# Second half of the attention product with V moved ahead of the FFN's value projection

## What is computed

```python
x = layernorm(x + causal_attention(x))          # 16 heads of 16, keys and queries of rank 32
x = layernorm(x + cross_attention(x, ctx))      # 120 context rows, masked after the softmax
x = layernorm(x + ffn(x))                       # r = sigmoid(xr @ W_r.T); k = relu(xk @ W_k.T)**2
                                                # out = r * (k @ W_v.T); xr, xk mix x with the row before
```

## Time and profile before

| | |
|---|---|
| median of 3 runs | 938.26 us (938.09 to 940.07) |
| the profiled execution | 941.16 us, its span from first to last instruction 939.5 us |
| busy share of the span | PE 94%, PEld 77%, DVE 72%, ACT 64%, POOL 47% |
| mean granted TensorE clock | 0.974 |
| chain that ended last | PE 84%, DVE 4%, issue 3%, POOL 2%, DMA 2%, ACT 2% |

### The profile page before, as it was taken

One profiled execution on the slowest core, in us unless ns is written; L12 is line 12 of the kernel. 1 busy time (PEld: TensorE's weight loads), 2 busy tenths in 40 slices (PEclk: granted clock), 3 DMA queues, 4 the chain that ended last, 5 costly groups with the idle time before them and its releaser, 6 DMA issues.

```text
span 939.5 us, 25990 instructions
## 1 busy us (share of the span) xinstructions
PE 883.4 (94%) x9686; PEld 727.9 (77%) x9686; DVE 677.5 (72%) x1565; ACT 598.3 (64%) x1153; POOL 438.7 (47%) x665
## 2 busy tenths in 40 slices
PE   4679899999999999999999999999999999988985
PEld 4557688888888888888888888888888888877765
DVE  2345777778878778777887877877788787776542
ACT  1114467766667667776666766777666676667643
POOL 3001345455455545545545554545545555444553
PEclk8779999999999999999999999999999999999998
DMA  7987667788766667778876667678887676551000
GB/s 210 157 149 137 131 129 138 153 155 155 135 105 134 142 138 141 140 154 156 153 125 111 141 134 143 139 143 154 155 154 109 116 151 137 124 78 29 27 12 23
DMA packets 121880, 120.14 MB, mean 128 GB/s; under 512 B 28249, under 2 KB 105243, under 8 KB 121627
## 3 DMA queue, kind: packets, MB, share of 16 engines
q1 hardware_dynamic: 121755, 118.47, 65.6%
HBM read 75.05 MB, written 42.99 MB: 126 GB/s over the span
## 4 chain that ended last, share of the span: by engine, by line
PE 84%; DVE 4%; issue 3%; SPq 2%; POOL 2%; DMA 2%; ACT 2%; ACTq 0%; POOLq 0%; DVEq 0%
PE ps_m L514 21%; PE ps_m L506 14%; PE ps_s L527 9%; PE ps_o L608 9%; PE ps_t L527 6%; PE ps_s L540 4%; PE ps_m L477 4%; PE ps_m L664 4%; PE ps_m L486 3%; PE ps_m L694 3%; PE ps_m L681 3%; PE ps_m L494 3%; PE ps_t L540 1%; DVE row_max L932 1%; DMA x_in<-in_x_turned 1%
## 5 line engine op out<-in xcount | busy, mean ns | idle before, releaser
L932 DVE TENSOR_REDUCE row_max<-ps_s 128x4 f32<-128x1024 f32 (+1 forms) x192 | 234.8, 1223 | 117.0 <-PE ps_s L540 114.7
L732 ACT ACTIVATE p<-ps_t 128x1024 f32<-128x1024 f32 x192 | 196.3, 1022 | 48.0 <-PE ps_t L540 47.7
L1115 POOL TENSOR_TENSOR xT_lo<-x_in,xT_hi 128x512 fp32r<-128x512 f32 x32 | 42.5, 1329 | 181.6 <-ACT xT_hi L719 181.6
L527 PE MATMUL ps_s<-stack 51*128 51x128 f32 (+1 forms) x1024 | 107.9, 310 | 10.2 <-DVE row_max L932 5.0
L527 PEld LDWEIGHTS ps_s<-stack 51*128 51x128 f32 x1024 | 72.4, 188 | 43.9 <-issue 15.3
L608 PE MATMUL ps_o<-p,v_pad 128*32 128x256 f32 (+1 forms) x2048 | 97.4, 331 | 0.2 <-ACT p L732 0.2
L841 ACT COPY kxT<-ps_m 128x240 f32<-128x240 f32 x32 | 11.5, 358 | 132.8 <-PE ps_m L486 132.8
L527 PE MATMUL ps_t<-stack 53*128 53x128 f32 (+1 forms) x1024 | 91.5, 278 | 2.8 <-DMA stack<-shift_dram 1.4
L608 PEld LDWEIGHTS ps_o<-p,v_pad 128*32 128x32 f32 x2048 | 58.0, 110 | 39.7 <-issue 17.9
L1140 POOL TENSOR_TENSOR var<-mv,eps 128x2 f32<-128x2 f32 x96 | 18.7, 195 | 146.4 <-DVE mv L955 145.7
L527 PEld LDWEIGHTS ps_t<-stack 53*128 53x128 f32 x1024 | 73.9, 189 | 4.8 <-ACT p L732 2.2
(11 more groups left out here) (168 smaller groups left out, 2689.9 us busy)
## 6 DMA issues: line engine op xcount, KB each, us to landing
stack<-parts_dram SPq DMA_DIRECT2D x384, 128.0 KB, 5.7
parts_dram<-parts SPq DMA_DIRECT2D x64, 512.0 KB, 6.0
x_in<-in_x_turned SPq DMA_DIRECT2D x32, 256.0 KB, 8.2
x_res<-in_x SPq DMA_DIRECT2D x32, 256.0 KB, 5.5
out_x<-sum SPq DMA_DIRECT2D x64, 128.0 KB, 6.4
ctxT<-in_ctx_turned SPq DMA_DIRECT2D x32, 120.0 KB, 5.4
shift_dram<-shift_turned SPq DMA_DIRECT2D x64, 16.0 KB
stack<-shift_dram SPq DMA_DIRECT2D x64, 16.0 KB
```

What stands on the lines that cost most here:

```text
L527: nc.tensor.matmul(target[:, at_h:at_h + width], left[b.slot][r0:r0 + rows_n, h // 2, rows_at:rows_at + P], right[b.slot][r0:r0 + rows_n, ...
L732: nc.scalar.activation(p[c][:], ps_t[:], ACT.Exp).then_inc(exp_done[c], 1)
L932: nc.vector.tensor_reduce(row_max[:, :, j0:j0 + nj, tile], ps_s[:].rearrange("p (g j w) -> p g j w", j=nj, g=2), AX_X, ALU.max) \
L1115: g.tensor_tensor(xT[b.slot][1][:], x_in[:], xT[b.slot][0][:].bitcast(F32), ALU.subtract) \
```

## The change

On TensorE `PV(1)` moves from behind z2 to behind g, that is past v3 and z2. On VectorE `attention_out(1)` moves from the end of the step to directly behind `attention_out(0)`, that is past `gated`, `sum2` and the statistics of `sum2`. On ScalarE the rounding `yT_hi` moves from the beginning of the next step to the end of the same step, ahead of the copies of kx and vx. Nothing is added to the work or taken from it.

```diff
                     last.then_inc(filled["f_g"], 1)
                 filler(7, ffn_last)
+                PV(1)
                 if on[FFN]:
                     bank = bank_free(pe, "v3", at)
...
                 filler(16, cross_last)
-                PV(1)
                 if on[PROBS]:
                     bank = bank_free(pe, "kx", at)
...
-                if on[CROSS]:
-                    act.wait_ge(y_turned[0], X.n + 1)
-                    act.wait_ge(y_turned[1], X.n + 1)
-                    wait(act, filled["f_z1"], X.n)
-                    nc.scalar.copy(flat(yT[0]), flat(y32T)).then_inc(a_["yT_hi"], 1)
                 X1, F1 = Batch(at - 1, CROSS), Batch(at - 1, FFN)
                 exp(0)
...
                 x_hi(at + 1)
+                if on[PROBS]:
+                    act.wait_ge(y_turned[0], Pb.n + 1)
+                    act.wait_ge(y_turned[1], Pb.n + 1)
+                    wait(act, filled["f_z1"], Pb.n)
+                    nc.scalar.copy(flat(yT[0]), flat(y32T)).then_inc(a_["yT_hi"], 1)
                 if on[PROBS]:
                     act.wait_ge(filled["f_kx"], Pb.n + 1)
...
                 attention_out(0)
+                attention_out(1)
                 if on[FFN]:
                     dve.wait_ge(filled["f_v3"], F.n + 1)
...
                 if on[CROSS]:
                     stats(1, X, sum2, v_["sum2_done"])
-                attention_out(1)
```

## The result

| | before | after |
|---|---|---|
| median of 17 runs each | 938.81 us (936.80 to 948.12) | 947.66 us (944.81 to 954.28) |
| ratio of the two, 95% interval | | 1.0087 [1.0070, 1.0105] |
| the profiled execution, its span | 941.16, 939.5 us | 948.0, 946.3 us |
| mean granted TensorE clock | 0.974 | 0.978 |
| one step in the steady part, from kx to kx | 26.14 us | 26.42 us |

The change makes the kernel 0.87% slower by the ratio, 8.2 us on 938.8; the two medians are 8.9 us apart. The spans of two single profiles differ by the set-up as well (the first kx starts between 80.5 and 84.1 us, in no relation to the kernel), so lengths are compared from kx to kx: the start of the last kx stands 810.9 us behind that of the first before (83.8 to 894.7) and 820.3 after (81.5 to 901.7).

The account below looks back on a forecast made before the run. The prediction took TensorE's row of products to bound the kernel. Per step, 0.10 us won at v3 less 0.41 us of new wait at kx gave +0.31; 29 x 0.31 = 9.0 on 938.26 made 947.3 us, range 944 to 953.

Parts of the forecast that it names:

- The wait that it named: On TensorE ahead of kx: a new wait for `gated` to read v3's bank, 0.41 us a step.
- The 0.10 us at v3: On TensorE: v3 no longer waits for `r_tanh`, since `PV(1)` covers it, worth -0.10 us a step.
- VectorE's row: On VectorE: `attention_out(1)` starts at 423.84, then `gated` follows at 425.67 and ends at 426.36.
- The term of 0.31 us a step: At kx: 0.10 us won at v3 less 0.41 us of new wait gives +0.31 a step, bounds +0.21 to +0.43.
- What was held to be covered: vx's wait for `sum2` covered by 0.3 us, `offset` by 1.3, `yT_lo` by 1.4; the earlier `yT_hi` costs nothing.
- Step 4: The step without v3: expected within -0.2 to +2 us and taken at nothing.
- The sum: Over steps 5 to 33: 29 x 0.31 = 9.0 us, added to 938.26 to give 947.3 us.
- The base of 938.26: The median time of the kernel before, in us, to which the forecast added 9.0 us.
- kx wouldn't wait, or hardly: Two rivals at kx: no wait, 935.4 us down to 932.5, chance 0.06; wait about 0.10 us, 936.4 to 940.1, chance 0.05.
- The meeting with GpSimd: Rival: VectorE's second `y` meets `xT_lo`, up to 0.64 us more a step, up to 966 us; chance 0.06.
- the loss might sit in TensorE's order or ScalarE's move: Rivals named with the experiments: TensorE's new order itself costs, or earlier `yT_hi` holds ScalarE; no chance given.

Follow-up runs that it names:

- turn_behind: The changed kernel with only the last transpose of the second half moved behind `gated` on VectorE: 938.79 us, 0.9981 of before.
- dose_after: The changed kernel with a memset of an unused 128x512 tile on VectorE directly ahead of the wait for v3: 965.96 us, 1.0266 of before.
- dose_before: The kernel before the change with a memset of an unused 128x512 tile on VectorE directly ahead of the wait for v3: 940.32 us, 0.9998 of before.
- port_meeting: The changed kernel with a 128x2 power on GpSimd ahead of `xT_lo`, so that it meets the second multiply `y`: 955.39 us, 1.0161 of before.
- yT_hi_back: The changed kernel with the rounding `yT_hi` put back to the start of the next step on ScalarE: 950.10 us, 1.0085 of before.
- pe_alone: The kernel before with only TensorE's move of `PV(1)` ahead of v3, VectorE and ScalarE left as they were: 945.85 us, 1.0066 of before.
- gated_first: The changed kernel with `gated` put ahead of `attention_out(1)` on VectorE again: 1003.74 us, 1.0669 of before.
- rest_alone: The kernel before with only VectorE's and ScalarE's moves, `PV(1)` still behind z2 on TensorE: 1072.81 us, 1.1401 of before.

## Why the prediction was right

The forecast was 947.3 us, and the median is 947.66. The wait that it named is there, in the place and nearly of the size that it gave; that the total came within 0.4 us is luck in part, as the sum below shows. Set off by 2.24 us (g starts at 423.36 instead of 421.12), the prediction's own chain stands beside the trace:

| instruction | forecast | trace of after |
|---|---|---|
| `PV(1)` | 422.08 + 2.24 = 424.32 | 424.31 |
| v3 | 425.76 | 425.75 |
| z2 | 427.28 | 427.28 |
| first of `attention_out(1)` | 426.08 | 426.07 |
| its last transpose | 427.54 | 427.53 |
| `gated` | 427.91 | 427.89 |
| kx | 428.65 | 428.60 |

- *The 0.10 us at v3* was right: the wait for `r_tanh` is gone, and with the new wait taken away as well, in turn_behind, kx stands 0.11 us closer to g than before.
- *VectorE's row* was right to 0.02 us; the back-to-back distances of 0.37 and 1.46 us, read in a step without FFN, held in the steady part.
- *The term of 0.31 us a step* was a little too large. `gated` took 0.65 us, not the 0.69 of the earlier trace rows, and kx came 0.05 us earlier than forecast. From g to kx pass 5.24 us instead of 4.98; the step is 0.28 longer, and 29 x 0.28 = 8.1 us instead of 9.0.
- *What was held to be covered* was covered. vx follows kx without a wait in the steady part; `yT_hi` runs at 428.05, ahead of the copy of kx; and `yT_lo` runs right behind `offset` and waits for nothing of ScalarE's, as the timeline of GpSimd in after shows:

```profile
431.44 0.19 POOL L1146 TENSOR_TENSOR offset<-neg_mean,rstd 128x2 f32<-128x2 f32 x1
431.58 1.28 POOL L1154 TENSOR_TENSOR yT_lo<-y32T,yT_hi 128x512 fp32r<-128x512 f32 x1
```

- *Step 4* was taken at nothing, within -0.2 to +2, and at full granted clock it costs 1.6 us: from g to the next step's first slot pass 7.73 us in dose_after (103.83 to 111.56) and 6.12 in dose_before (102.12 to 108.24). Both have the order of after and of before there, and no dose, since step 4 has no FFN. The profiles of after and before can't be set against each other in this step, because TensorE ran a part of it at half rate in each: 8.67 us in after (102.55 to 111.22, granted clock 0.87), 7.75 before (106.60 to 114.35, 0.78). What waits there is vx, not kx: `sum2` now stands behind both halves in that step too. vx in step 4, by the timeline of TensorE, first in after and then in dose_after:

```profile
109.22 2.06 PE L494 MATMUL ps_m<-T_Wxv,ctxT 128*120 128x256 f32 x4 [2.19 <-DVE sum L1060]
```

```profile
110.50 1.12 PE L495 MATMUL ps_m<-T_Wxv,ctxT 128*120 128x256 f32 x4 [2.19 <-DVE sum L1062]
```

- *The sum.* The term put in 0.9 us too much over 29 steps and step 4 was left out with 1.6, so the parts come to 8.1 + 1.6 = 9.7 us, against 9.0 forecast and 8.2 (6.6 to 9.9 by the interval) or 8.9 measured. The base of 938.26, a median of 3 runs, lies 0.55 us under that of 17. These errors nearly cancel, and nothing in the prediction made them do so.
- *The rivals.* That kx wouldn't wait, or hardly, is refuted by the trace. The meeting with GpSimd is real but lies 0.25 us away in after; port_meeting brought it about and it cost 0.28 us a step. That the loss might sit in TensorE's order or ScalarE's move is settled by turn_behind and yT_hi_back, which keep both or undo one.
- *What the prediction did not see* is how little of the change makes the loss, and what TensorE's part does by itself: it looked only forward from the moved pieces to the next reader of a bank, and not at the next step's exps, which are queued behind `yT_hi` on ScalarE. In after that doesn't matter; in pe_alone it is the whole loss.

## What to carry to other kernels

Where two products take turns in a bank, count the cover in time on both engines: what stands on the writer's side between the bank's last product and the next one, and what stands on the reader's side ahead of the read. A move that takes a short wait from the front of such a chain can use up the cover at its end, here 1.5 us for a gain of 0.10; and a piece that is moved on a reading engine need not go whole, since the one instruction that nobody waits for yet can stay behind the read. When an engine's work is moved earlier, look in the same way at what its unmoved rest does to the next step.

## What the runs showed of the hardware

- The granted clock of TensorE answers to waits of quite different lengths. With an empty 0.29 us a step it stayed at 1.00 through the steady part; with 1.53 us in a step of 27.83 (gated_first) a stretch at half rate came in about every fourth step; with 2.64 us in a step of 30.5 (rest_alone) the stretch behind the wait shown above was granted 0.54, which is nearly all at 1.2 and not 2.4 GHz, while one step of the same run with the same wait stayed at 1.00. In step 4 an empty 2.19 us ahead of vx was followed by half rate in after and in yT_hi_back (vx took 2.06 us) and by full rate in dose_after and gated_first (1.12 us). What decides between these is not settled by the runs.
- A VectorE multiply with two inputs in SBUF that begins while GpSimd runs a subtraction or an addition on SBUF ends 0.28 us behind the GpSimd instruction, in each of the three places shown: in port_meeting (430.24 against 429.96), in gated_first (418.89 against 418.61) and in step 4 of before. The Trainium skill (SBUF — State Buffer, section "SBUF: two separate sides") says that the second of two such instructions is blocked for the whole of the first. The trace agrees in so far as `y` never ends before the other; of the 0.42 us that it takes alone, 0.28 are left behind the other's end. The price here is 0.26 to 0.68 us, by how early `y` comes.
- The write of zeros on VectorE began 0.50 us behind the start of the transpose ahead of it, where the reads of PSUM began 0.36 to 0.37 us behind it. Why is open.
